# GNN layer with neighbour gathers: at most two indirect gathers under way at a time

## The reference

```python
mask = adj != 0
scores = where(mask, -arange(N), -inf)
vals, idx = top_k(scores, 25)                 # the first 25 neighbours
feats = where(vals > -inf, x[idx], -inf)      # 25 rows of 256
agg = feats.max(axis=2)
agg = where(degree <= 25, maximum(agg, 0), agg)
out = relu(concat([x, agg]) @ W + b)
return layernorm(x + out)
```

## Time and profile before

| what | us |
|---|---|
| median of 3 runs | 3765.63 |
| lowest and highest run | 3760.57, 3766.75 |
| the profiled execution, its own time | 3760.97 |
| its span, first to last instruction | 3759.2 |
| GpSimd busy, of the span | 2077.1 |
| of that, the 1920 gathers of 15 per tile | 2035.5 |
| DVE busy, of the span | 2335.7 |
| TensorE matmuls busy, of the span | 2407.7 |

### The profile page before, as it was taken

One profiled execution on the slowest core, in us unless ns is written; L12 is line 12 of the kernel. 1 busy time (PEld: TensorE's weight loads), 2 busy tenths in 40 slices (PEclk: granted clock), 3 DMA queues, 4 the chain that ended last, 5 costly groups with the idle time before them and its releaser, 6 DMA issues.

```text
span 3759.2 us, 47488 instructions
## 1 busy us (share of the span) xinstructions
PE 2407.7 (64%) x15529; PEld 1575.3 (42%) x15728; DVE 2335.7 (62%) x5090; ACT 1294.2 (34%) x2441; POOL 2077.1 (55%) x2078
## 2 busy tenths in 40 slices
PE   4664666664666766666766666646676766766664
PEld 2443434443444444444444444434444444444432
DVE  4665656655656656666656666656665766656665
ACT  4332333332333333333333333323333333333331
POOL 3554555554555555555555555555555555555554
PEclk8876777876778676777677777767766776677776
DMA  3554564555644565455555555555565555554554
GB/s 139 133 116 90 121 149 116 130 119 90 140 131 114 118 132 135 120 129 113 120 147 117 120 130 116 138 107 115 117 132 134 120 133 113 121 135 117 133 96 74
DMA packets 172601, 457.65 MB, mean 122 GB/s; under 512 B 42817, under 2 KB 92482, under 8 KB 154882
## 3 DMA queue, kind: packets, MB, share of 16 engines
q0 software_dynamic: 93600, 255.72, 38.4%
q1 hardware_dynamic: 78690, 198.31, 15.2%
HBM read 436.47 MB, written 16.78 MB: 121 GB/s over the span
## 4 chain that ended last, share of the span: by engine, by line
another core or an unknown queue 38%; DVE 21%; PE 18%; issue 11%; ACT 10%; POOL 2%; DMA 0%; DVEq 0%; POOLq 0%; ACTq 0%
PE near_ps L640 13%; DVE got L756 6%; ACT sign L428 5%; PE z_ps L615 2%; POOL got L395 2%; DVE key_left L791 1%; DVE word_top L793 1%; DVE word_top L788 1%; ACT numbered L467 1%; DVE got L850 1%; DVE got L856 1%; ACT limit L462 1%; DVE cand L768 1%; DVE top L802 1%
## 5 line engine op out<-in xcount | busy, mean ns | idle before, releaser
L395 POOL DMA_INDIRECT got<-in_x,index x1920 | 2035.5, 1060 | 1596.7 <-DVE index L773 910.1
L640 PE MATMUL near_ps<-parts,hot 128*128 128x256 bf16 x7152 | 1366.5, 358 | 675.7 <-issue 426.2
L640 PEld LDWEIGHTS near_ps<-parts,hot 128*128 128x128 bf16 x7152 | 865.9, 125 | 1126.1 <-issue 598.4
L756 DVE TENSOR_REDUCE got<-near_ps 128x256 f32<-128x2048 f32 (+6 forms) x376 | 692.0, 1840 | 441.0 <-remote 402.2
L467 ACT ACTIVATE numbered<-bits_ps 128x256 f32<-128x256 f32 x128 | 49.1, 384 | 1479.0 <-remote 1479.0
L783 DVE SCALAR_TENSOR_TENSOR key<-bits_ps,numbered 128x256 f32<-128x256 f32 x128 | 54.3, 424 | 722.2 <-ACT numbered L467 713.9
L660 PE MATMUL out_ps<-w_sb,h_t 128*128 128x256 f32 x1024 | 356.0, 508 | 0.0
L579 PE MATMUL z_ps<-mask_t,later_b 128*34 128x128 bf16 x2048 | 197.2, 272 | 219.5 <-ACT mask_t L432 183.3
L850 DVE TENSOR_TENSOR got<-got 128x2304 f32<-128x2304 f32 (+1 forms) x128 | 322.7, 2521 | 16.0 <-DMA got<-in_x,index 13.3
L457 ACT ACTIVATE val<-z_ps,rank_col 128x1024 int16<-128x1024 f32 x256 | 284.5, 1111 | 93.0 <-PE z_ps L615 72.9
L856 DVE TENSOR_TENSOR got<-got 128x1024 f32<-128x1024 f32 (+2 forms) x384 | 299.9, 781 | 13.2
(11 more groups left out here) (114 smaller groups left out, 1971.1 us busy)
## 6 DMA issues: line engine op xcount, KB each, us to landing
adj_sb<-in_adj_turned SPq DMA_DIRECT2D x128, 1024.0 KB
got<-in_x,index POOLq DMA_INDIRECT x1920
x_sb<-in_x SPq DMA_DIRECT2D x128, 128.0 KB
h_t<-in_x_turned SPq DMA_DIRECT2D x128, 128.0 KB
out<-result SPq DMA_DIRECT2D x128, 128.0 KB
heads<-in_x_near SPq DMA_DIRECT2D x8, 1536.0 KB, 10.8
w_sb<-in_L_gnn_W SPq DMA_DIRECT2D x1, 512.0 KB
hot<-vacant SPq DMA_DIRECT2D x32, 4.8 KB
```

The source lines that it names most:

```text
L395: pool.indirect_dma_start(out=to, out_offset=None, in_=x_rows, in_offset=bass.IndirectOffsetOnAxis(ap=at, axis=0)).then_inc(landed, 16)
L640: mm = pe.matmul(near_ps[:, s - k * ROUND:s - k * ROUND + 1, :], hot[:, a.i, s * P:(s + 1) * P], parts[:, (a.side * PARTS + n) * CH + c, N ...
L756: dve.tensor_reduce(got[:, a.i, FAR + k, :], near_ps[:, 0:n, :].rearrange("p q c -> p c q"), AX.X, ALU.max).then_inc(near_used, 1)
```

## The change

Gathers 0, 2, 4, ... 14 of a tile count on `landed[0]`, gathers 1, 3, ... 13 on `landed[1]`. Before gather s (from s = 2 on) GpSimd waits until gather s-2 has landed, and after the last it waits until both semaphores have the tile's full counts, before it loads the flag. `landed_of(a, side, n)` is the value of a semaphore at which n gathers of its side have landed in tile a.T. DVE's `combine` waits for both. Nothing that is computed or moved changes.

```diff
@@ -274,6 +274,10 @@
+        def landed_of(a, side, n):
+
+            return (16 * ((FAR + 1 - side) // 2)) * a.T + 16 * n
@@ -402,7 +406,13 @@
                 pool.wait_ge(agg_ready, done(a.T - 2))
                 pool.sem_inc(far_begun, 1)
                 for s in range(FAR):
-                    gather(got[:, a.i, s, :], index[:, a.i, s:s + 1], gathered[a.i])
+                    if s > 1:
+                        pool.wait_ge(landed[s % 2], landed_of(a, s % 2, s // 2))
+                        pool.sem_inc(far_begun, 1)
+                    gather(got[:, a.i, s, :], index[:, a.i, s:s + 1], landed[s % 2])
+                for side in range(2):
+                    pool.wait_ge(landed[side], landed_of(a, side, (FAR + 1 - side) // 2))
+                    pool.sem_inc(far_begun, 1)
                 pool.wait_ge(flag_ready, done(a.T))
@@ -831,7 +841,8 @@
                 dve.wait_ge(near_used, rounds_done(a.g, a.t, ROUNDS[a.t] - 1))
-                dve.wait_ge(gathered[a.i], (16 * FAR) * in_pairs(a.g, a.t) + 16 * FAR)
+                for side in range(2):
+                    dve.wait_ge(landed[side], landed_of(a, side, (FAR + 1 - side) // 2))
                 dve.sem_inc(rows_at_vec, 1)
```

More of the change, by code:

```diff
@@ L213, in build @@
         more_done = sem("more_done")
-        gathered = [sem(f"gathered{i}") for i in range(2)]
+        landed = [sem(f"landed{i}") for i in range(2)]
         near_ready = sem("near_ready")
```

## The result

The changed kernel takes 4799.8 us (median of 4 runs, 4794.3 to 4801.8) against 3766.2 us before in the same measurement: 1.274 times as long, with a 95% interval of 1.272 to 1.277. The forecast was 4725 us. The profiled execution has a span of 4797.6 us.

What follows compares the result with a forecast made beforehand. The TensorE, ScalarE and DVE ring bounds the kernel at 28.07 us a tile; GpSimd's 35.7 us cycle takes over. 942 us (124 tiles), 12 (overflow) and 9 (last tile) add 963 to 3761.0: 4725 us, range about 4300 to 5230.

Steps and rivals of the forecast that it cites:

- Hand-over: GpSimd, start of gather s to s+2: latency plus 0.83 us restart, 3.53 us early, 4.43 late; seven per tile.
- Rival A: Not slower: hand-overs stay hidden if their mean is below 3.27 us; 3762 us, chance 4%.
- Late places: Late gathers of a tile, mostly reading the same padding row: latency 3.6 us, four hand-overs of 4.43 us.
- SP's loads: SP's loads share the DMA engines with the gathers: 1.0 us more per tile, taken between 0 and 4.5.
- DVE's stretch: One gather per tile is lengthened beside DVE's 128x2304 maximum: 1.45 us more.
- Last landing and end: End of a tile's gathers on GpSimd: last landing 3.6 us, then 1.3 us to the next tile's first gather.
- The cover of the indices: DVE needs 25.7 us from combine to the indices two tiles on, so they are ready 10 us early.
- Overflow tiles: Three tiles with ten extra gathers: 65.3 us each instead of 61.4, 3.9 more each.
- B: Far slower: late gathers keep 5.7 us latency even with two in flight; cycle 46.2 us, 6040 us, chance 7%.
- C: The change doesn't do what it says, waits pass early: 3761 us, chance 1%.
- D: Faster: less crowding lets SP's loads land earlier; 3750 us at best, chance 1%.
- a ring period of 28.07 us: Tile period of the kernel before, set by TensorE, ScalarE and DVE waiting on each other, with slack for gathers.

Runs made afterwards that it cites:

- when doubled: Changed kernel, with SP loading each tile's 1 MB of adjacency a second time into an unused buffer: 5037.3 us.
- unrolled control: Changed kernel with GpSimd's loop written out so that every wait is against a constant, same increments behind the waits: 4789.4 us.

## Why the prediction was right, and where it missed

The forecast was right in sign, size and mechanism: GpSimd's cycle became the bound. Two things in its closeness are luck: errors inside the sum that cancel, and a measurement at the level of the trace it was worked out from (both below). Step by step:

- **Hand-over.** 3.53 us for early places; the median from place 1 to 3 and from 2 to 4 is 3.56. Less the restart of 0.8 that is a latency of some 2.8 us, and 3.5 to 3.6 for late places. Rival A needed 3.27 in the mean; of all hand-overs from s to s+2 the shortest is 3.44, so it fell. By the Trainium skill, "DMA: Bandwidth & Descriptors", section "Anatomy of one DMA — SWDGE (gpsimd) path", 2.0 us plus bytes over 436 GB/s, 128 KB take an estimated 2.3 us; this case's gathers do not agree, with 2.8 us at early places.
- **Late places.** 4.43 x 4 = 17.7; the last four even hand-overs have means of 4.03, 4.04, 4.21 and 4.45, in sum 16.7. The slow kind sets in gradually instead of at once. The pairs that were forecast dissolve by it: the last distances are 1.9 and 2.6 us in turn, not 1.25 and a gap.
- **SP's loads.** 1.0 us was too little. The hand-over that meets them is 5.53 beside 3.8 and 4.0, so 1.6, and 1.8 per MB when doubled. DVE's stretch was sized at 1.45 and is 0.8 now that it falls on the first gather (1.79 us in the mean, against 0.95), which makes the first hand-over 4.37. These errors cancel: 30.8 us expected from place 0 to 14, 30.4 measured.
- **Last landing and end.** 3.6 + 1.3 expected; 4.0 + 1.4 to 1.5 measured. From first gather to maximum 34.4 us expected, 34.4 the median; period 35.7 expected, 35.8 the median. The prediction took the maximum's start for the landing. In the changed kernel's chain the landing itself comes 0.4 us earlier (a gather started at 2332.82 lands after 3.56, the maximum starts at 2336.80, the next gather at 2338.46).
- **The cover of the indices.** The prediction gave DVE 25.7 us from a maximum to the next index, so 10 us to spare. It takes 17.7 here (median), and 19.8 are to spare: the 25.7 held waits of the old ring, which have gone (DVE's key waited 713.9 us for ScalarE, now 62.8). This helped nothing and cost nothing, since GpSimd's cycle is the bound either way.
- **Overflow tiles.** 65.3 us expected, the three longest distances between first gathers are 65.1, 65.4 and 66.1. Before they were 58.6, 59.9 and 61.4: the prediction took the first, which is the longest, for all three.
- **What was missing** is in the mean, 36.9 instead of 35.8 + 0.7 for the overflow tiles. The last tile of a graph, for which the sum had no term of its own, takes 42.2 us (median). Two costs come together there, as the timeline of the changed kernel shows (a graph's last tile):

```profile
2411.22 2.06 POOL L399 DMA_INDIRECT got<-in_x,index  x1 [4.72 <-issue]
...
2422.78 0.21 SPq L310 DMA_DIRECT2D heads<-in_x_near  x1
2425.76 0.95 POOL L399 DMA_INDIRECT got<-in_x,index  x1 [2.57 <-DMA got<-in_x,index]
...
2429.81 0.95 POOL L399 DMA_INDIRECT got<-in_x,index  x1 [3.10 <-DMA got<-in_x,index]
...
2449.00 2.56 DVE L861 TENSOR_TENSOR got<-got 128x2304 f32<-128x2304 f32 x1 [19.57 <-DMA got<-in_x,index]
2453.24 1.12 POOL L399 DMA_INDIRECT got<-in_x,index  x1 [7.31 <-issue]
```

The load of `heads` for a later graph, 1.5 MB, draws places 0 to 14 out to 33.8 us (2411.22 to 2444.99) from some 30.3. The seventh graph has no such load at its end, and there the places take 30.0. And between maximum and next gather stand 4.24 us instead of 1.4: GpSimd's loop jumps back there. In the unrolled control the same place has 2448.22 to 2449.51, 1.29 us. Against 35.7 the seven graph ends take 42 us more in all, of the 75 by which the forecast was low. Another 21 are 0.18 us in each of the 117 other tiles (mean 35.88), and the rest lies in the overflow tiles, which before were shorter than taken, and in rounding.

- **The other rivals.** B (late gathers keep 5.7 us with two in flight) is refuted by the late hand-overs of 4.4 us, so a latency near 3.6, with one and with two under way; C (the waits don't hold) by the shortest hand-over, 3.44 us where it was 2.5, and the 985 waits for landings in the table; D by the result.

What the prediction took for a property of the kernel, a ring period of 28.07 us, holds at one level only. The changed kernel, in its unrolled form, is within 0.3% of 4800 us beside the faster one; the ratio is 1.27 here and 4789 / 3084 = 1.55 for the unrolled form there. The forecast of 25% more would have been far off beside that level, though its 4725 us would not. What puts the kernel before at one level or the other is open.

## What to carry to other kernels

A limit on transfers in flight sets a pitch (the time from one to the next) of (latency + restart) / limit, longer where another load is in the way. Read latency and restart from the trace, the restart from a wait of the same form, and compare the pitch with what the consumer needs; with two under way and 3.5 to 4.4 us a hand-over the pitch was 1.8 to 2.2 us against 1.25, with three it almost fitted. A wait at the end of a batch costs even when the waits inside are free (1.151 against 0.999 here), because the last landing and the restart then stand open. And slack that you read in one trace may be gone in the next measurement of the same kernel: profile it again before you spend it.

## What the runs showed of the hardware

- Gathers in which many nodes read the same row are slow by themselves: a late hand-over of 4.4 us became 3.5 with distinct rows, and 16 padding rows in place of one cut the gather queue's share of the DMA engines from 38.4% to 22.5% for the same bytes.
- A wait on the gather itself restarts it 0.26 us after the landing, a wait with an increment behind it 0.79 us after: 4384 against 4789 us for the whole program.
- GpSimd's jump back at the end of its loop cost 2.8 us where its queue had run empty (4.24 against 1.29 us unrolled), and nothing in the kernel before, where it had not (a period of 27.8 us there too).
- The same program took 3728 to 3766 us (granted clock near 0.74) in some measurements and 3080 to 3084 (near 0.83) in others, and kept to its level within each. The changed kernel took 4800 us beside the slower level and its unrolled form 4789 beside the faster.
